# GpSimd clears first, first weights loaded in halves, and the first turns laid out anew in a fused attention and feed-forward kernel

## What is computed

```
x = L0_attn_x                                   # [16, 256, 256], f32
h = layernorm(x)
q, k, v = h @ wq.T, h @ wk.T, h @ wv.T          # 16 heads of 16
s = q k^T / 4, -inf where j - i > 16
x = x + (softmax(s) v) @ wo.T
h = layernorm(x)
gate_w, up_w = spline(gate_cp), spline(up_cp)   # [1024, 256] each
down_w = spline(down_cp)                        # [256, 1024]
x = x + (silu(h @ gate_w.T) * (h @ up_w.T)) @ down_w.T
```

## Time and profile before

| | us |
|---|---|
| median of 3 runs | 597.4 (597.32 to 599.65) |
| the profiled execution | 596.52 |
| its span | 594.8 |
| PE busy | 573.7 (96%) |
| VectorE busy | 509.4 (86%) |
| ScalarE busy | 243.3 (41%) |
| GpSimd busy | 204.4 (34%) |

### The profile page before, as it was taken

One profiled execution on the slowest core, in us unless ns is written; L12 is line 12 of the kernel. 1 busy time (PEld: TensorE's weight loads), 2 busy tenths in 40 slices (PEclk: granted clock), 3 DMA queues, 4 the chain that ended last, 5 costly groups with the idle time before them and its releaser, 6 DMA issues.

```text
span 594.8 us, 13700 instructions
## 1 busy us (share of the span) xinstructions
PE 573.7 (96%) x5376; PEld 497.9 (84%) x5376; DVE 509.4 (86%) x1031; ACT 243.3 (41%) x369; POOL 204.4 (34%) x247
## 2 busy tenths in 40 slices
PE   3898899999999999999999999999999999999997
PEld 1465578899898888989888898989888888988897
DVE  6788799999988899998989999999998998886552
ACT  1324445433533444443443444344444434343422
POOL 4432444233323334224232333324242423333432
PEclk9979999999999999999999999999999999999999
DMA  8531312212222221131312122132211112101000
GB/s 239 133 123 58 118 45 91 94 50 73 90 73 76 73 68 56 55 107 56 108 56 92 40 67 72 57 107 74 89 56 48 53 64 72 55 19 37 2 19 18
DMA packets 44143, 42.86 MB, mean 72 GB/s; under 512 B 4528, under 2 KB 42544, under 8 KB 44080
## 3 DMA queue, kind: packets, MB, share of 16 engines
q1 hardware_dynamic: 44080, 41.99, 22.5%
HBM read 12.35 MB, written 4.19 MB: 28 GB/s over the span
## 4 chain that ended last, share of the span: by engine, by line
PE 91%; DVE 4%; issue 1%; DMA 1%; ACT 1%; POOL 1%; SPq 0%; DVEq 0%
PE ring L727 15%; PE ring L728 13%; PE ring L729 13%; PE ring L805 9%; PE ring L734 8%; PE pair L773 7%; PE ring L735 7%; PE ring L736 7%; PE pair L797 5%; PE ring L718 2%; PE ring L751 2%; PE pair L782 1%; DMA POWER<-powers 1%; DVE M L662 1%; PE ring L788 1%
## 5 line engine op out<-in xcount | busy, mean ns | idle before, releaser
L563 ACT ACTIVATE P<-pair 128x800 f32<-128x800 f32 x128 | 106.3, 837 | 129.2 <-PE pair L797 128.8
L727 PE MATMUL ring<-YT,WGUh 128*128 128x256 f32 x512 | 151.6, 296 | 0.0
L729 PE MATMUL ring<-YT,WGUl 128*128 128x256 f32 x512 | 144.3, 282 | 0.0
L728 PE MATMUL ring<-YT,WGUh 128*128 128x256 f32 x512 | 144.1, 281 | 0.0
L662 DVE TENSOR_REDUCE M<-pair 128x2 f32<-128x288 f32 (+1 forms) x256 | 134.3, 570 | 4.8 <-PE pair L782 1.1
L519 POOL TENSOR_TENSOR IN<-GU,IN 128x512 fp32r<-128x512 f32 x64 | 83.4, 1304 | 134.1 <-ACT IN L524 134.0
L727 PEld LDWEIGHTS ring<-YT,WGUh 128*128 128x128 f32 x512 | 96.3, 188 | 6.9 <-issue 2.2
L728 PEld LDWEIGHTS ring<-YT,WGUh 128*128 128x128 f32 x512 | 96.6, 189 | 0.0
L729 PEld LDWEIGHTS ring<-YT,WGUl 128*128 128x128 f32 x512 | 96.2, 188 | 0.0
L511 POOL TENSOR_SCALAR_AFFINE_SELECT P<-P 128x448 f32<-128x448 f32 x64 | 37.8, 590 | 161.9 <-ACT P L563 161.7
L656 DVE TENSOR_TENSOR pair<-pair,UP 128x512 f32<-128x512 f32 x104 | 71.4, 686 | 9.1 <-PE pair L773 9.0
(11 more groups left out here) (80 smaller groups left out, 1064.7 us busy)
## 6 DMA issues: line engine op xcount, KB each, us to landing
QM<-QK SPq DMA_DIRECT2D x96, 128.0 KB, 2.1
KS<-QK SPq DMA_DIRECT2D x96, 128.0 KB, 2.1
X<-x SPq DMA_DIRECT2D x32, 256.0 KB, 3.0
out<-X SPq DMA_DIRECT2D x16, 256.0 KB, 2.3
OVER<-over SPq DMA_DIRECT2D x4, 256.0 KB, 8.5
P<-wqk SPq DMA_DIRECT2D x1, 512.0 KB, 4.4
TAP<-points SPq DMA_DIRECT2D x2, 256.0 KB, 6.3
POWER<-powers SPq DMA_DIRECT2D x2, 256.0 KB, 7.0
```

The lines of the kernel that those rows point to most:

```text
L563: nc.scalar.activation(P[:, g % 2, 2 * (n % 2):2 * (n % 2) + 2, :], pair(what, t, n)[:, :, 0:SW], ACT.Exp, scale=SCALE).then_inc(exp_done, 1)
L727: mm(o, wh[:, kb, c], act[:, 0, kb, :], start=j == 0 and kb == 0, stop=False, skip_group_check=True)
L728: mm(o, wh[:, kb, c], act[:, 1, kb, :], start=False, stop=False, skip_group_check=True)
L729: i = mm(o, wl[:, kb, c], act[:, 0, kb, :], start=False, stop=False, skip_group_check=True)
```

## The change

- The second slot's clears (`fill` 3 and 4) go from VectorE to GpSimd, and the list now begins with `fill` 0 and 1, so that GpSimd starts with the two clears of slot 0, and `la` and `lb` of turn 0 follow at once. `ld` waits for four clears on GpSimd from turn 1 on, instead of two there and three on VectorE.
- The weights of query and key are loaded as two transfers of 256 KB with a semaphore each; points and powers of the first piece and the rows go between them.
- The tables START and OWN of turns 0 to 2 are new; in the others a few numbers differ by small amounts. From the fifth turn or so to the fifteenth the list is the same but for a few neighbours that change places.

```diff
-START = [("raw", 0, 1, 1, -1124.762, 0), ("split", 0, 1, 1, -995.456, 0), ("fill", 0, 1, 1, -955.165, 0),
...
+START = [("fill", 0, 1, 1, -415.818, 0), ("fill", 1, 1, 1, -313.266, 0), ("raw", 0, 1, 1, -223.498, 0),
...
-        raw_loaded = [sem(f"raw_loaded{j}") for j in range(3)]
+        raw_loaded = [sem(f"raw_loaded{j}") for j in range(4)]
...
-                    sp.dma_start(raw(0, 2), wqk.rearrange("(k p) c -> p k c", p=128)).then_inc(raw_loaded[0], DMA)
-                    sp.dma_start(ROWS[:], rows.rearrange("r (a p) -> r a p", a=2)).then_inc(rows_loaded, DMA)
+                    def query_key(n):
+                        c = slice(n * D, (n + 1) * D)
+                        sp.dma_start(raw(0, 2)[:, :, c], wqk.rearrange("(k p) c -> p k c", p=128)[:, :, c]).then_inc(raw_loaded[n], DMA)
+
+                    query_key(0)
                     for j in PIECES:
                         c = slice(j * 512, (j + 1) * 512)
                         for dst, src in ((TAP, points), (POWER, powers)):
                             sp.dma_start(dst[rows_in(j), c], src[rows_in(j), c]).then_inc(points_loaded[j], DMA)
+                        if j == 0:
+                            sp.dma_start(ROWS[:], rows.rearrange("r (a p) -> r a p", a=2)).then_inc(rows_loaded, DMA)
+                            query_key(1)
                         sp.dma_start(OVER[:, c], over[:, c]).then_inc(over_loaded[j], DMA)
...
-                    sp.wait_ge(cleared, 2)
-                    if t:
-                        sp.wait_ge(filled, 3)
+                    sp.wait_ge(cleared, 4 if t else 2)
...
-                elif what == "fill" and n < 2:
-                    dst, value = ((KS, 1.0), (QM, 0.0))[n]
-                    nc.gpsimd.memset(dst[:, 0, :, :].bitcast(F32), value).then_inc(cleared, 1)
+                elif what == "fill" and n != 2:
+                    slot = n // 3
+                    dst, value = ((KS, 1.0), (QM, 0.0))[n - 3 * slot]
+                    nc.gpsimd.memset(dst[:, slot, :, :].bitcast(F32), value).then_inc(cleared, 1)
...
-                    act.wait_ge(raw_loaded[max(n - 1, 0)], DMA)
+                    act.wait_ge(raw_loaded[n], DMA)
...
-                elif what == "fill" and n > 2:
-                    dst, value = ((KS, 1.0), (QM, 0.0))[n - 3]
-                    nc.vector.memset(dst[:, 1, :, :].bitcast(F32), value).then_inc(filled, 1)
```

More of the change, by code:

```diff
@@ L100, in steps @@
     return [(what, n + by * i, at + gap * i) for what, n, count, by, at, gap in table for i in range(count)]
-START = [("raw", 0, 1, 1, -1124.762, 0), ("split", 0, 1, 1, -995.456, 0), ("fill", 0, 1, 1, -955.165, 0),
[L104 to L108, removed]
[11 rows of a table removed]
-OWN = {0: [("la", 0, 1, 1, -969.356, 0), ("ld", 0, 1, 1, -665.9, 0), ("lb", 0, 1, 1, -623.228, 0),
[69 rows of a table removed]
+START = [("fill", 0, 1, 1, -415.818, 0), ("fill", 1, 1, 1, -313.266, 0), ("raw", 0, 1, 1, -223.498, 0),
+             ("tap", 0, 1, 1, -192.468, 0), ("fill", 2, 1, 1, -189.098, 0),
[13 rows of a table added]
+OWN = {0: [("la", 0, 1, 1, -258.964, 0), ("lb", 0, 1, 1, -228.564, 0), ("zt", 0, 1, 1, -187.18, 0),
[63 rows of a table added]
              ("zt", 0, 1, 1, -38.137, 0), ("qk", 0, 2, 1, -24.208, 15.3056),
@@ L202 @@
              ("ld", 0, 2, 1, -10.158, 27.5538), ("xr", 0, 1, 1, 2.435, 0),
[1 row of a table removed]
[1 row of a table added]
              ("sc", 0, 8, 1, 40.86, 3.9714), ("av", 0, 4, 1, 50.129, 9.0736),
              ("ot", 0, 2, 1, 74.748, 3.4615), ("on", 0, 1, 1, 82.886, 0),
[1 row of a table removed]
[1 row of a table added]
              ("z2", 0, 1, 1, 147.392, 0), ("ga", 0, 4, 1, 168.719, 25.3974),
              ("up", 0, 4, 1, 174.162, 24.7127), ("ic", 0, 4, 1, 217.204, 10.5805),
[3 rows of a table removed]
[3 rows of a table added]
              ("ld", 0, 2, 1, -3.5, 12.0393), ("s1", 0, 8, 1, 2.863, 4.6009),
[3 rows of a table removed]
[3 rows of a table added]
              ("xr", 0, 1, 1, 224.833, 0), ("mb", 0, 1, 1, 245.912, 0), ("z2", 0, 1, 1, 253.544, 0),
              ("ga", 0, 4, 1, 322.906, 32.8609), ("up", 0, 4, 1, 340.612, 44.6215),
[1 row of a table removed]
[1 row of a table added]
              ("y", 0, 1, 1, 733.252, 0)]}
-TURN = [("x", 0, 1, 1, -70.71, 0), ("la", 0, 1, 1, -58.13, 0), ("lb", 0, 1, 1, -44.728, 0),
+TURN = [("x", 0, 1, 1, -70.71, 0), ("la", 0, 1, 1, -58.13, 0), ("lb", 0, 1, 1, -44.635, 0),
              ("zt", 0, 1, 1, -38.138, 0), ("qk", 0, 2, 1, -24.209, 15.3056),
@@ L438, in _ @@
                             sp.dma_start(dst[rows_in(j), c], src[rows_in(j), c]).then_inc(points_loaded[j], DMA)
+                        if j == 0:
+                            sp.dma_start(ROWS[:], rows.rearrange("r (a p) -> r a p", a=2)).then_inc(rows_loaded, DMA)
+                            query_key(1)
                         sp.dma_start(OVER[:, c], over[:, c]).then_inc(over_loaded[j], DMA)
                         if j == 0:
-                            sp.dma_start(raw(2, 1), wv.rearrange("(k p) c -> p k c", p=128)).then_inc(raw_loaded[1], DMA)
-                            sp.dma_start(raw(3, 1), wo.rearrange("(k p) c -> p k c", p=128)).then_inc(raw_loaded[2], DMA)
+                            sp.dma_start(raw(2, 1), wv.rearrange("(k p) c -> p k c", p=128)).then_inc(raw_loaded[2], DMA)
+                            sp.dma_start(raw(3, 1), wo.rearrange("(k p) c -> p k c", p=128)).then_inc(raw_loaded[3], DMA)
                     for dst, src in ((UP, upper), (IDB, identb)):
```

## The result

The changed kernel takes **591.57 us** (median of 20 runs, 590.4 to 597.94), the kernel before 597.44 (20 runs beside them, 595.64 to 605.55). The ratio is 0.9895, 95% interval 0.9875 to 0.9915: faster by 1.05%, or by 5.9 us from median to median. The forecast was 599.2 with a range from 593.3 to 602.5. The profiled execution took 592.19 us, its span is 590.5.

A forecast was written before the change was run, and what follows sets the result against it. The prediction took TensorE's matmuls as the bound, with only the start able to change the time. Span 594.8 + 5.2 (later first matmul) - 3.4 (clock) = 596.6, with 2.6 from span to median 599.2 us; range 593.3 to 602.5.

The forecast's parts named there:

- What bounds the kernel: Whole kernel: TensorE's steady part is full of matmuls; only the start, up to 80 us, changes the time.
- Part 1: First loads: points ahead of the second half of wqk let the first matmul start at 8.2, 1.7 us earlier.
- Part 2: Two clears leave VectorE, 1.76 us each; the second one's 1.76 come off where PE waits for VectorE.
- The hold: Start of VectorE: a normalization beside a running GpSimd instruction waits for it, ending about 0.15 us after a GpSimd instruction.
- Part 3: GpSimd's start: ISA at 6.1 us and blocked normalizations delay the first matmul to 15.1, +5.2 us.
- Part 4: New order behind the start: the clock's 3.4 us saved, 10 to 80 us idle time unchanged; bounds 0 and 6.9.
- The fall of the clock: PE from 31 to 38 us: a backlog leaves the drop in clock without a cause, saving 3.4 us.
- (a): GpSimd's start: ISA costs nothing, first matmul at 8.2 to 9.7, 594.0 us measured; chance 0.27.
- (b): Start: ISA at full size and the low clock returns or stays, so 3.4 isn't saved: 602.6 us; chance 0.13.
- (c): GpSimd's start: ISA costs 1.3 us, first matmul at 10.3, +0.4, 594.4 us measured; chance 0.10.

The follow-up runs named there:

- the probe: Kernel before with one tiny GpSimd TENSOR_TENSOR added right behind the instruction named ISA; a single execution took 596.8 us.
- The order alone: Changed kernel with the second slot's clears back on VectorE and the first loads as before: 596.4 us, ratio 0.9942 to the kernel before.
- one moved qk: Changed kernel with the second qk of turn 0 behind four of the ten spline matmuls instead of all ten: 599.8 us, ratio 1.0004 to the kernel before.
- order and clears: Changed kernel with the first loads as before, clears left on GpSimd: 592.9 us, ratio 0.9881 to the kernel before.
- order and halves: Changed kernel with the second slot's two clears back on VectorE: 595.7 us, ratio 0.9944 to the kernel before.

## Why the prediction was wrong

**What bounds the kernel** held: the steady part moved by 0.45 us of idle time, the rest of the difference lies before 80 us.

**Part 1** held in its mechanism. The half of wqk was copied from 5.82 on, 0.8 later than forecast, which changed nothing behind it. The powers landed at 7.9 instead of 7.4, so the first matmul came at 8.76 against the 8.2 of this part: 1.2 us earlier than before instead of 1.7. In the two traces with the same course of the clock the halves were worth these 1.2.

**Part 2** held in the sum and not as a mechanism. In the new order the two clears are worth 1.0 to 1.3 us at 0.991 and 0.5 to 0.6% over all executions; in the old one they cost 2. The part priced only the engine that loses the work. The hold, which the prediction itself read in the earlier trace rows, also has to be priced on the engine that gets it.

**Part 3 is the step that failed.** ISA was put at 6.1 us, the upper bound, with the reason that its own row's surroundings are nearest. They measured the wait for ScalarE. It costs less than 0.1 us (the probe at 0.98). With it fell everything built on it: RSTD came at 4.89 instead of 10.6, the normalizations ended at 6.35 instead of 14.4, the first matmul came at 8.76 instead of 15.1. In the sum: +5.2 was forecast, -1.2 measured, 6.4 us. The row that should have weighed more was there: an idle stretch that ends 0.2 us behind the very releaser that the profile names is explained by that releaser, and nothing is left over for a second cause. The page's rule that was quoted beside it (the Trainium skill, "GPSIMD Engine Reference", on wrapper-ucode dispatch, a load of 5.95 us) speaks of the first call to a freshly loaded kernel, a condition that the prediction left out. It doesn't carry over to this ISA ahead of a plain TENSOR_TENSOR: less than 0.1 us in the probe.

**Part 4** had two terms, both wrong, in opposite directions. The fall of the clock was put at -3.4. It did not come back, and neither did a second one from 58.5 to 61.9, which the part had not priced (1.7). But the first rise came at 32.9 instead of 20.9, so that PE worked 24.1 us ahead of it instead of 11.0, and that costs 6.6. Together PE's busy time rose by 1.5: missed by 4.9. The idle time from 10 to 80 was taken as unchanged and fell from 7.0 to 1.85, 5.15 us: this is the mis-sized term that carries most of the gain. The upper bound of the part, 3.4 + 3.5 saved, took in half of the idle time. PE has a backlog there, as the part says; but what a backlog takes away in every trace of the new order is the idle time, while the clock takes a different course in each, and the sum had it the other way round. The order alone has the small idle time (0.57 us from 10 to 50), and one moved qk takes it away (4.95).

**The sum by its terms.** Span forecast 596.6, measured 590.5, -6.1: start -6.4, clock and busy time +4.9, idle 10 to 80 -5.15, steady part and tail +0.5. The offset from span to median was taken as 2.6 and is 1.1 here (591.57 - 590.5), another -1.5; 1.7 of it lies between the span and the time of one and the same execution in both kernels, and the rest is chance, where the profiled execution lies among the others. Together -7.6, from 599.2 to 591.6.

**The rivals.** (a) was the true case of ISA: RSTD 4.9, pair early, first matmul from 8.2 to 9.7. Its time, 594.0, was still 2.4 too high, and that it came so near is in part luck. It had the idle time of 10 to 80 rise by 1.0 where it fell by 5.15, the clock's 3.4 come back where 1.5 were lost, and the offset 1.5 too high; the first two errors of 6.15 and 4.9 nearly cancel. Had its range reached down by the 3.5 of idle time that Part 4 names as a bound, it would have held the result. (b) and (c) rested on ISA and fell with it.

**The clock is what no order here commands.** The order alone rose at 50 us in its profiled execution, order and clears at 34.0, the changed kernel at 32.9, order and halves at 17.5 with a fall at 20.9. What decides it is open in these runs; its price is that executions of one kernel differ by 3 us and more, those of the kernel before by up to 10.

## What to carry to other kernels

When an instruction without a duration stands in an idle stretch, look at the releaser: if the work behind it starts within the usual delay of that releaser, nothing says that the instruction costs anything, and a probe of one tiny instruction settles it. When an order is laid out anew, price the idle time that its backlog can remove before the clock, and look for what each long run of one engine covers on the others, and for matmuls that overlap only while they stand beside each other. Before work moves from VectorE to GpSimd, look for a TENSOR_SCALAR of VectorE that would run beside it.

## What was not expected of the hardware

- A TENSOR_SCALAR of VectorE is held by GpSimd's work also when it is tiny: 128x2 took 2.80 us instead of 0.17, and 1.06 in the changed kernel (28.84), where it ended at 29.90 with a TENSOR_TENSOR of GpSimd (29.87). A TENSOR_TENSOR can stand beside a clear: the tap at 7.92 in the changed kernel took its usual 0.69 while GpSimd cleared KS. But the tap shown below took twice that, beside two TENSOR_TENSORs of GpSimd (21.42 to 24.36), and the second of these took 1.68 instead of 1.27. The kernel with the second qk earlier has the same again (1.25 and 1.70). The spline sums, which read PSUM, kept their 0.69 beside GpSimd's TENSOR_TENSORs; whether that is the difference was not tested.
- 40 dense matmuls from 1.25 us on bring PE to 2.4 GHz by the first spline matmul (1.09 instead of 2.04 us); it is at 1.2 GHz again from 20 to 30 us, while PE is 96% busy.
- Two spline matmuls of 32 rows beside each other took 2.08 us at the low clock, one alone 2.07.
- Where nothing has been recorded, the clock column reads 1.00 though matmuls take 0.41 instead of 0.28 us.

VectorE and GpSimd of the changed kernel near 22 us:

```profile
21.86 1.39 DVE L604 TENSOR_TENSOR TAP<-TAP,POWER 128x512 f32<-128x512 f32 x1
```

```profile
21.42 1.28 POOL L479 TENSOR_TENSOR WQKl<-P,WQKh 128x512 fp32r<-128x512 f32 x1
22.68 1.68 POOL L503 TENSOR_TENSOR WGUl<-W,WGUh 128x512 fp32r<-128x512 f32 x1
```
